# Convolution, attention and routed experts on one core: GpSimd's distance step moved to VectorE, picks and scalings rescheduled

## The reference, cut to what matters

```python
x = x + conv(group_norm(x))                     # deformable convolution: 8 groups of 32 channels, 9 points
t = t + slice_attention(layer_norm(t))          # 8 heads, 32 slices
t = t + experts(layer_norm(t))                  # 8 experts of 128 -> 512 -> 128, the best two of each token
...
samp = gather(y0, x0) * (wy0 * wx0) + gather(y0, x0 + 1) * (wy0 * wx1) + ...   # bilinear, positions from x
out = einsum('bhwgkc,bhwgk->bhwgc', samp, weights)
```

## Time and profile before

| what | us |
|---|---|
| median of 3 runs | 1287.29 (1287.22 to 1292.36) |
| the profiled execution | 1296.12 |
| its span, first to last instruction | 1294.4 |
| start, before the first product of the loop | 52.4 |
| the loop of 320 slots with its last projection | about 52 to 1130 |
| tail (attention and experts of the last image) | about 1130 to 1294 |

### The profile page before, as it was taken

The page is one execution under the profiler, slowest core; times in us unless marked ns, Lnnn a source line. Parts: engine busy times, 40 slices in busy tenths (PEclk is TensorE's granted clock), DMA queues, the critical chain, the costliest instruction groups (busy, mean ns, idle before and its releaser), DMA issues.

```text
span 1294.4 us, 50786 instructions
## 1 busy us (share of the span) xinstructions
PE 983.0 (76%) x22310; PEld 797.5 (62%) x22310; DVE 829.0 (64%) x1652; ACT 773.6 (60%) x1432; POOL 687.0 (53%) x652
## 2 busy tenths in 40 slices
PE   4487785877688776899778766998877657777984
PEld 3465564656457665787457555887466546646984
DVE  5766757686856864656766855556668847555454
ACT  2676665767657663576767663666667554345552
POOL 2564545565544576453865584445745695200474
PEclk9689797988889886899998987999798878988997
DMA  6703130132000032364211212453110321163813
GB/s 169 154 24 53 43 79 24 68 56 68 25 24 25 24 109 83 89 187 117 62 46 33 74 60 77 141 167 107 48 47 25 97 68 46 41 177 95 258 48 98
DMA packets 142781, 104.80 MB, mean 81 GB/s; under 512 B 43697, under 2 KB 125938, under 8 KB 142050
## 3 DMA queue, kind: packets, MB, share of 16 engines
q1 hardware_dynamic: 138242, 92.68, 26.3%
q0 software_dynamic: 4320, 8.86, 2.2%
HBM read 76.32 MB, written 25.19 MB: 78 GB/s over the span
## 4 chain that ended last, share of the span: by engine, by line
PE 50%; ACT 18%; DVE 17%; issue 9%; POOL 4%; DMA 2%; SPq 0%; DVEq 0%; POOLq 0%; ACTq 0%
PE ps L1025 14%; PE ps L1009 10%; ACT xsb L1395 7%; PE ps L1246 5%; PE ps L1033 5%; PE ps L1259 4%; DVE asb L1738 4%; ACT asb L1413 2%; ACT xsb L1389 2%; DVE xsb L1715 2%; DVE ysb L1729 2%; PE ps L1140 2%; DVE region L1991 2%; PE ps L965 2%; PE ps L1142 2%
## 5 line engine op out<-in xcount | busy, mean ns | idle before, releaser
L882 POOL TENSOR_TENSOR ysb<-ysb,rw 128x576 f32<-128x576 f32 x300 | 336.5, 1143 | 345.5 <-DVE ysb L1729 345.3
L1009 PE MATMUL ps<-xsb,ysb 64*64 64x96 f32 x11008 | 326.3, 269 | 123.8 <-DVE asb L1738 30.8
L1009 PEld LDWEIGHTS ps<-xsb,ysb 64*64 64x64 f32 x11008 | 277.2, 149 | 184.7 <-issue 96.8
L1395 ACT ACTIVATE xsb<-xsb,pick 128x576 f32<-128x576 f32 (+1 forms) x480 | 336.8, 751 | 5.2
L1738 DVE COPY asb<-ps 128x960 f32<-128x960 f32 (+1 forms) x208 | 215.7, 1043 | 120.0 <-PE ps L1025 110.2
L871 POOL TENSOR_TENSOR ysb<-rw,count 128x576 f32<-128x576 f32 (+1 forms) x150 | 175.6, 1171 | 74.5 <-PE ps L1009 73.8
L1025 PE MATMUL ps<-asb,vd 32*32 32x258 f32 x8192 | 185.9, 393 | 27.4 <-issue 17.0
L1404 ACT ACTIVATE osp<-ps 128x258 f32<-128x258 f32 x128 | 43.0, 443 | 251.3 <-PE ps L1025 251.3
L1025 PEld LDWEIGHTS ps<-asb,vd 32*32 32x32 f32 x8192 | 124.5, 104 | 78.4 <-issue 47.0
L1487 ACT ACTIVATE region<-ps,b_col 128x128 f32<-128x128 f32 x368 | 105.0, 369 | 88.6 <-PE ps L1246 88.4
L1715 DVE TENSOR_TENSOR xsb<-rw,ps 128x576 f32<-128x576 f32 (+1 forms) x150 | 108.0, 720 | 55.6 <-PE ps L1009 54.0
(11 more groups left out here) (308 smaller groups left out, 1193.1 us busy)
## 6 DMA issues: line engine op xcount, KB each, us to landing
ring<-in_L_ffn_W SPq DMA_DIRECT2D x122, 256.0 KB, 3.5
vd<-group_values SPq DMA_DIRECT2D x128, 128.0 KB, 2.7
set_rows<-ring SPq DMA_DIRECT2D x4, 1376.0 KB, 6.6
rw<-set_rows SPq DMA_DIRECT2D x30, 172.0 KB, 3.4
group_values<-region SPq DMA_DIRECT2D x32, 128.0 KB, 3.5
asb<-in_L_ffn_W SPq DMA_DIRECT2D x16, 256.0 KB, 5.6
region<-sorted_rows SPq DMA_DIRECT2D x6, 512.0 KB, 5.1
expert_rows<-region SPq DMA_DIRECT2D x6, 512.0 KB, 5.5
```

The costliest lines, as they stand in the source:

```text
L882: pl.tensor_tensor(ysb[:, ch % DEPTH, 0:sets, u, :], ysb[:, ch % DEPTH, 0:sets, NU - 1, :], rows_of(ig)[:, 2 + u, first:first + sets].rear ...
L1009: last = pe.matmul(ps[64 * j:64 * j + 64, bank + i, NV * GRID * q:NV * GRID * (q + 1)], ysb[rows, ch % DEPTH, col, :, :].rearrange("p u y ...
L1395: act.activation(xsb[:, ch % DEPTH, 0:sets, v, :], xsb[:, ch % DEPTH, 0:sets, NV - 1, :], ACT.Relu, bias=pick[:, v:v + 1], scale=-1.0).the ...
```

## The change

1. **y distances.** For chunks from the fourth on (`apart`), VectorE makes the y distances instead of GpSimd, right behind its x distances and from the same grid in PSUM. GpSimd is left with the weighing, the sorting and the picking.
2. **Picks and adds.** The 16 picks of images 0 and 1 are spread over 24 slots (89 to 112) instead of 12, and the adds go to slots 113 to 117. The late image keeps its slots.
3. **Scalings.** Of the six groups of sorted rows per image, VectorE scales the even ones and ScalarE the odd ones, with a semaphore for each.
4. **Slots.** Of the prepared images step 0 moves from slot 0 to 2, step 1 from 1 to 3 and step 2 from 5 to 6; in the attention of images 0 to 2 the square root (`std`) moves from slot 5 to 7 and `normalise` from 6 to 7.
5. **Load order.** The four loads of `outw` go behind the images' loads.

```diff
-PE_PREP = ((0, 0), (5, 2), (8, 3)) + ...
+PE_PREP = ((2, 0), (6, 2), (8, 3)) + ...
-ACT_PREP = (((0, 0), (8, 3)) + ...
+ACT_PREP = (((2, 0), (8, 3)) + ...
-DVE_PREP = (((1, 1), (5, 2), (9, 3), (10, 20), (11, 15))
+DVE_PREP = (((3, 1), (6, 2), (9, 3), (10, 20), (11, 15))
-ACT_STEPS = {5: ("std",), 9: ("tnT",), ...
+ACT_STEPS = {7: ("std",), 9: ("tnT",), ...
-DVE_STEPS = {3: ("stats",), 6: ("normalise",), ...
+DVE_STEPS = {3: ("stats",), 7: ("normalise",), ...
-PICK_SLOT, PICK_SLOTS = 89, 12
-ADD_SLOT, ADD_SLOTS = 101, 5
+PICK_SLOT, PICK_SLOTS = 89, 24
+ADD_SLOT, ADD_SLOTS = 113, 5
+LATE_PICK_SLOTS = 12
...
+def apart(ch):
+    return ch >= 3 and True
...
-                for j in range(4):
-                    load(outw[j * GC:(j + 1) * GC, :, :], ..., "conv")
             def load_other_weights():
+                for j in range(4):
+                    load(outw[j * GC:(j + 1) * GC, :, :], ...)
...
@@ GpSimd's loop
-                    if ch + 3 < ALL_CHUNKS:
+                    if ch + 3 < ALL_CHUNKS and not apart(ch + 3):
                         y_distances(ch + 3)
...
@@ ScalarE
+            def scale_rows(b, q):
+                if q % 2 == 0:
+                    return
+                act.wait_ge(s.columns_ready, b + 1)
+                act.wait_ge(s.tiles_turned, TURNS * b + q + 1)
+                for i in range(4 * q, min(4 * q + 4, ROWS)):
+                    last = act.activation(turned_rows(b, i), ps[:, 6 + q % 2, i % 4 * P:(i % 4 + 1) * P], ACT.Identity,
+                                          bias=shift_col[:, b % 2, i:i + 1], scale=scale_col[:, b % 2, i:i + 1])
+                last.then_inc(s.odd_scaled, 1)
...
@@ VectorE
+            def y_distances(ch, grid):
+                ig, first, sets = chunk_of(ch)
+                dve.tensor_tensor(ysb[:, ch % DEPTH, 0:sets, NU - 1, :],
+                                  rows_of(ig)[:, 1, first:first + sets].rearrange("p (s o) -> p s o", o=1)
+                                  .broadcast_to([P, sets, GRID]),
+                                  grid.rearrange("p (o q) -> p o q", o=1).broadcast_to([P, sets, GRID]),
+                                  ALU.subtract).then_inc(s.y_apart, 1)
...
             def scale_rows(b, q):
+                if q % 2:
+                    return
...
@@ VectorE's loop
                         x_distances(ch + 3, grid_of(bank))
+                        if apart(ch + 3):
+                            y_distances(ch + 3, grid_of(bank))
                     y_ramp(ch + 2, units_of(bank))
```

More of the change, by code:

```diff
@@ L64 @@
 TURN_PREP = tuple((31 + h, TURN + h) for h in range(TURN_STEPS))
[L65 to L66 removed]
+PE_PREP = ((2, 0), (6, 2), (8, 3)) + tuple((COLUMN_SLOTS[c], COLUMN + c) for c in range(COLUMN_STEPS)) + TURN_PREP
+ACT_PREP = (((2, 0), (8, 3)) + tuple((COLUMN_SLOTS[c], COLUMN + c) for c in range(1, NT))
             + ((23, SCALE), (27, 27)) + TURN_PREP)
[L68 removed]
+DVE_PREP = (((3, 1), (6, 2), (9, 3), (10, 20), (11, 15))
             + tuple((COLUMN_SLOTS[c], COLUMN + c) for c in range(COLUMN_STEPS))
@@ L135, in lifted @@
     return slot % 2 == 1 and (n < SLOTS or 8 < slot < 56)
+def apart(ch):
+    return ch >= 3 and True
+APART = [0]
+for _ch in range(ALL_CHUNKS):
+    APART.append(APART[-1] + apart(_ch))
 LIFTED = [0]
@@ L567, in load_other_weights @@
             def load_other_weights():
+                for j in range(4):
+                    load(outw[j * GC:(j + 1) * GC, :, :], t_in["L0_conv_out_w"].rearrange("(g c) o -> c g o", g=G))
                 load(wx_raw, t_in["L1_attn_W_x"].rearrange("(h p) c -> p h c", p=P))
@@ L860, in side @@
                     else:
-                        for m in share_of(at, pick_slot(b_), PICK_SLOTS, TOP * NT):
+                        for m in share_of(at, pick_slot(b_), PICK_SLOTS if b_ < LATE else LATE_PICK_SLOTS, TOP * NT):
                             pick_rows(b_, m)
@@ L1102, in wait_for_banks @@
                     for q in last_of([(TURN_ROWS_SLOTS[q], q) for q in range(TURNS)], at):
-                        pe.wait_ge(s.tiles_scaled, TURNS * image_no + q + 1)
+                        for earlier_q in range(max(0, q - 1), q + 1):
+                            wait_scaled(image_no, earlier_q)
                     for i in last_of([(tile_slots(image_no)[i], i) for i in range(ROWS + 1)], at):
@@ L1226, in turn_rows @@
                 elif q >= 2:
[L1227 removed]
+                    wait_scaled(b, q - 2)
                 for i in range(4 * q, min(4 * q + 4, ROWS)):
@@ L1493, in work @@
                     attend(b, step)
+                for q in turn_of(b, slot):
+                    scale_rows(b, q)
                 for i in gelu_of(b, slot):
@@ L1992, in scale_rows @@
                                              scale_col[:, b % 2, i:i + 1], shift_col[:, b % 2, i:i + 1], ALU.mult, ALU.add)
-                last.then_inc(s.tiles_scaled, 1)
+                last.then_inc(s.even_scaled, 1)
             def find_homes(q):
```

27 lines of the change are left out of this document (15 added, 12 removed).

## The result

| | kernel before | changed kernel |
|---|---|---|
| median of 20 runs each | 1292.49 us | 1302.48 us |
| ratio, 95% interval | | 1.0068 [1.0048, 1.0088] |
| profiled execution / its span | 1296.12 / 1294.4 | 1305.68 / 1303.9 |
| TensorE's mean granted clock in it | 0.891 | 0.877 |

The change makes the kernel about 9 us **slower**. On the 1287.3 us of the forecast the ratio gives 1296.1 us [1293.5, 1298.6], just above the range of 1266 to 1294. The forecast of 1279 was wrong in sign, and a time above 1293.7 had been given a chance of 0.14.

What follows compares the result with a forecast made beforehand. No engine is full; the loop from engine to engine inside a chunk sets the time. Terms 26 - 14 - 3 - 6 - 5 - 4 - 2 = -8 us take 1287.3 to 1279.3 us (-0.6%), range 1266 to 1294.

Steps and rivals of the forecast that it cites:

- y distances: cost, less blocking and sort gain: Moving y distances to VectorE: 26 us cost there, less 3 us of blocking and 14 us in the sort stretches.
- picks and adds: Adds leave slots 21 to 25 for 33 to 37, picks spread over 24 slots: gain 4 us, bounds -2 and 10.
- square root: Attention of images: square root at slot 7 no longer stands between gelus; gain 2 us, bounds -2 and 4.
- scalings: Before the experts, halves on VectorE and ScalarE: 1.7 us for each of three images, gain 5 us, bounds -3 and 10.
- preparation's slots: Loop starts about 3 us earlier, later transposes are covered at 1.5 us each: gain 6 us, bounds 0 and 7.
- The bound of 2 us: Worst case for picks and adds: all sixteen adds, 5.6 us, in the new place's chain, less what they free.
- The sort stretch: GpSimd sets the pace; its chunk falls from 7.1 to 5.9 us, gaining 14 us over three stretches, bounds 9 and 18.
- The cost of the y distances: New VectorE subtractions at 0.65 us, 40 of them counting: 26 us, 16 of it in image 0; bounds 20 and 51.
- the closed loop of rows 3: Preparation's column steps, image 0: VectorE works without pause and sets the pace; nearly all 25 uncovered subtractions count, 16 us.
- the 3 us for less blocking: Position steps and adds of picked rows run less held up by GpSimd: gain about 3 us, bounds 0 and 7.
- VectorE becomes the bound: Rival: nearly all 79 uncovered y distances delay the take, cost 51 us, 1304 us; slower by over 0.5%: chance 0.14.
- all 79: The new VectorE subtractions not covered by idle time, out of 157; all counting would cost 51 us, 40 were taken.

Runs made afterwards that it cites:

- y_only: Kernel before with only the y distances on VectorE from the fourth chunk, and the load order; 1311.97 us, ratio 1.0082 to the kernel before.
- undo_y: Changed kernel with GpSimd making all y distances again; 1286.66 us, ratio 0.9937 to the kernel before.
- undo_scal: Changed kernel with all scalings on VectorE again; 1316.53 us, ratio 1.0167 to the kernel before.
- no_y_picks_std: Changed kernel without its y distances, picks and adds, and square root parts; 1275.81 us, ratio 0.9822 to the kernel before.
- undo_picks: Changed kernel with picks in slots 89 to 100 and adds in 101 to 105 again; 1293.23 us, ratio 0.9992 to the kernel before.
- sort_y: Kernel before plus shared scalings, preparation's slots, load order, and VectorE's y distances in sort stretches of images 1 to 3 only; 1265.73 us, ratio 0.9757.

## Why the prediction was wrong, by its steps

The value of a part is the ratio with it less the ratio without it, on 1292 us.

| step | forecast, us | measured, us |
|---|---|---|
| y distances: cost, less blocking and sort gain | 26 - 3 - 14 = +9 | +17 ± 5 (alone +11 ± 5) |
| picks and adds | -4 | +10 ± 6 |
| square root | -2 | +4 ± 5 |
| scalings | -5 | -13 ± 6 (alone -8 ± 4) |
| preparation's slots | -6 | -9 ± 5 |
| sum | -8 | +9 (measured as a whole: +9 ± 3) |

**Picks and adds is the step that failed most**: "They leave slots 21 to 25, where softmax and sums wait for VectorE, for slots 33 to 37, where ScalarE leads". I priced the place left and not the place taken, and put the wait that goes with the adds at nothing: the last pick is issued one slot before them, and VectorE stands 3.74 us for its rows. Behind that wait stand the router's statistics, the distances and the take, and slots 30 to 40 grew by 9.9 and 9.3 us. The part measured +10 us instead of -4, and without the wait the 10 us are gone. The bound of 2 us was for the adds alone, although the trace of the kernel before shows the wait with 3.85 us. These 14 us of error are the largest. The others (y distances +8, square root +6, scalings -8, preparation -3) come to +3 together only because they cancel, which is luck.

**The sort stretch** was overrated in size. Its mechanism was right: chunk 5.77 us, TensorE's wait halved. The gain of 14 us measured 6 to 7, below my bound of 9. I multiplied one well-read stretch by all chunks of it; slots 50 to 60 did gain 10.7 us, and slots 40 to 50 gave 4.8 back, from a cause that stays open.

**The cost of the y distances** held in size: 13.5 us in image 0 and 8.9 in the others, 22 against 26 - 3 = 23 (10.7 and 8.1 in y_only). In image 0 the closed loop of rows 3 is the cause, as told. In images 1 to 3 the size is in part luck, since most of it fell where I held the subtractions covered. Of the 3 us for less blocking, the three position steps give 1.3: 1706 to 1612 ns x 6, 1004 to 586 ns x 6, and 1111 to 1687 ns x 3 the other way. The Trainium skill (SBUF — State Buffer, "SBUF: two separate sides") says that a VectorE instruction with two SBUF inputs and a GpSimd instruction that reads SBUF shut each other out, and that the one that started first goes to its end. The means alone don't show it, but the single instructions agree. The first pair is the edge-weight step (two SBUF inputs) in the kernel before, the second the same step in the changed kernel, the last line the same step with GpSimd idle:

```profile
135.58 1.04 DVE L1687 SCALAR_TENSOR_TENSOR region<-region 86x864 f32<-86x864 f32 x1
135.61 2.04 POOL L871 TENSOR_TENSOR ysb<-rw,count 128x576 f32<-128x576 f32 x1
```

```profile
132.56 3.25 POOL L891 TENSOR_TENSOR ysb<-ysb,rw 128x576 f32<-128x576 f32 x2 [5.91 <-DVE ysb L1768]
134.72 2.00 DVE L1714 SCALAR_TENSOR_TENSOR region<-region 86x864 f32<-86x864 f32 x1
...
296.11 1.05 DVE L1714 SCALAR_TENSOR_TENSOR region<-region 86x864 f32<-86x864 f32 x1 [0.58 <-ACT region L1367]
```

Where VectorE starts 0.03 us ahead it takes 1.04 us and GpSimd's y distances 2.04 instead of their usual 1.17. Where GpSimd's weighing is under way it is VectorE that takes 2.00 instead of 1.05. So what the change gained here hung on which of the two came first, and I had counted a gain for every step.

**The scalings** were underrated by 3 to 8 us: ScalarE's first scaling comes before its ramps and not behind them, and the first expert tile starts 3.4 us sooner behind the first scaling instead of 1.7. **The preparation's slots** were right in sign and near in size. **The square root** has the wrong sign in its middle value, within the interval.

Of the rivals, the outcome lies in the time of "VectorE becomes the bound". Its sign came true: TensorE's waits for the take doubled, by the y distances alone in y_only and by the adds as well in the changed kernel (63.0 us against 47.4 with them back). But its size did not: the y distances cost about what the forecast had for 40 of them, and not the 51 us of all 79.

## What to carry to other kernels

Moving a step costs what it delays at its new slot, so walk the same chain there as at the old one, and keep a consumer several slots behind the last DMA that it needs. Relieving an engine pays only in the stretches where it sets the pace: all y distances on VectorE cost 11 to 17 us, and those of the sort stretches alone go with the fastest kernel, by a gain of 8 ± 8 us. A change of many parts is worth taking apart, since here parts worth +31 and -22 us hid behind a sum of +9.

## What the runs showed of the hardware that was not expected

**TensorE's clock decides a group's length by up to 9 us, and it differs from execution to execution.** The stretches below are slots 10 to 20 of images 1, 2 and 3: start:end, length, busy time and instructions of PE, PEld, DVE, ACT and POOL, granted clock, DMA share, GB/s. First before, then after.

```profile
347.00:383.00 36.00, 28.75 (x642) 16.84 (x635) 23.15 (x29) 22.84 (x37) 16.36 (x15) 0.91 0.08 22
627.00:659.00 32.00, 25.05 (x636) 15.88 (x632) 22.11 (x28) 22.71 (x35) 27.77 (x28) 1.00 0.19 51
907.00:948.00 41.00, 33.41 (x645) 18.20 (x641) 22.68 (x28) 23.27 (x36) 29.91 (x29) 0.83 0.16 43
```

```profile
354.00:396.00 42.00, 38.54 (x648) 21.64 (x642) 25.86 (x33) 23.15 (x36) 10.91 (x10) 0.67 0.07 19
635.00:672.00 37.00, 30.36 (x652) 17.55 (x642) 25.77 (x33) 23.17 (x36) 17.31 (x17) 0.86 0.13 35
922.00:956.00 34.00, 27.65 (x652) 17.06 (x644) 25.68 (x33) 23.23 (x37) 17.38 (x17) 0.95 0.15 38
```

The number of matmuls is the same within 3%, ScalarE is as busy in each and VectorE as busy within each kernel; the length follows the clock column. It does so across all kernels here, with or without any part of the change: 41.6 to 42.2 us at 0.67 to 0.68 (changed kernel, undo_y, undo_scal, no_y_picks_std), near 38 at 0.82, near 34 at 0.95 and 33 at 1.00; only the 41.0 at 0.83 stands off it. A finer cut of image 1, TensorE alone, first the changed kernel, then undo_picks:

```profile
348.00:360.00 12.00, 10.37 (x412) 0.99 0.17 48
360.00:364.00 4.00, 2.20 (x34) 0.72 0.00 0
364.00:388.00 24.00, 23.97 (x190) 0.50 0.03 9
```

```profile
348.00:360.00 12.00, 10.06 (x408) 1.00 0.16 48
360.00:364.00 4.00, 2.06 (x35) 1.00 0.02 4
364.00:388.00 24.00, 19.82 (x457) 1.00 0.04 10
```

What TensorE did before the third row is the same in both within 0.3 us of busy time in each stretch; then one goes through the attention's products at 0.50, the level of 1.2 GHz, without a pause, and the other at 1.00, the level of 2.4 GHz, with room left, and gets further in the same 24 us (457 matmuls instead of 190). The same matmuls, from the attention's first (L1154) to the projection (L1042), take 23.8 us in one (362.95 to 386.76) and 14.8 in the other (362.83 to 377.61), counted to the projection's start. So the 8 us by which slots 10 to 20 of image 1 differ is no effect of the picks, and a difference in one profiled execution is read with its clock beside it. The Trainium skill (TensorE: Matmul & The Clock Gate, "What's actually happening") says that how many matmuls run at the lower level varies between runs of one kernel. It says so of a kernel's start; these two traces, of different kernels but of the same work in this stretch, agree in kind and show it 350 us into the kernel.

The spread of single runs goes with it too. Over 27 runs of the kernel before on one chip the time falls by 5.5 us for each 0.01 of mean granted clock (correlation -0.79), from 1302.7 us at 0.873 to 1284.6 at 0.895. The changed kernel's mean over its runs is 0.882 against 0.886, so some 2.5 of its 9 us go with the clock, and sort_y's is 0.900, so some 8 of its 31. How far the clock is cause there and how far it follows TensorE's shorter waits, no run separates.
